# Scores of a short tile of 65 keys, made as two tiles of 64 columns, in a two-layer Perceiver kernel

## The reference

```python
q = (x @ Wq.T).reshape(B, N, H, D)
k = (y @ Wk.T).reshape(B, L, H, D)
v = (y @ Wv.T).reshape(B, L, H, D)
attn = jnp.einsum('bnhd,blhd->bhnl', q, k)
attn = jax.nn.softmax(SCALE * attn, axis=-1)
out = jnp.einsum('bhnl,blhd->bnhd', attn, v).reshape(B, N, C)
return out @ Wp.T + bp
```

## Time and profile before

| | |
|---|---|
| runs | 1291.32, 1292.21, 1295.77 us |
| median | 1292.21 us |
| profiled execution | 1284.61 us |
| its span (first to last instruction) | 1282.8 us |
| mean granted TensorE clock | 0.952 of full speed |
| busy | PE 90%, PEld 67%, DVE 49%, ACT 33%, POOL 26% |

### The profile page before, as it was taken

The page is one execution under the profiler, slowest core; times in us unless marked ns, Lnnn a source line. Parts: engine busy times, 40 slices in busy tenths (PEclk is TensorE's granted clock), DMA queues, the critical chain, the costliest instruction groups (busy, mean ns, idle before and its releaser), DMA issues.

```text
span 1282.8 us, 34101 instructions
## 1 busy us (share of the span) xinstructions
PE 1153.2 (90%) x15663; PEld 864.1 (67%) x15664; DVE 634.2 (49%) x977; ACT 426.2 (33%) x806; POOL 338.9 (26%) x366
## 2 busy tenths in 40 slices
PE   6888979796999999999999999999999999654986
PEld 3343434385788888887888887888887887442863
DVE  2011368546214555555555555556555545555286
ACT  1010152214224334334434434434334334221332
POOL 0000000104001333333333333233233233349122
PEclk9999989799999999999999999999999999766999
DMA  9999970633012002001002002002001003100000
GB/s 352 373 397 352 378 282 0 225 106 108 1 38 67 19 23 67 18 23 67 18 23 68 19 23 67 18 23 68 18 23 56 30 23 120 56 2 17 1 2 33
DMA packets 38879, 115.67 MB, mean 90 GB/s; under 512 B 2504, under 2 KB 3016, under 8 KB 34640
## 3 DMA queue, kind: packets, MB, share of 16 engines
q1 hardware_dynamic: 38736, 113.50, 24.6%
HBM read 112.44 MB, written 1.05 MB: 88 GB/s over the span
## 4 chain that ended last, share of the span: by engine, by line
PE 75%; DVE 8%; ACT 5%; SPq 5%; DMA 4%; issue 2%; POOL 0%; DVEq 0%; POOLq 0%; ACTq 0%
PE SB L389 45%; PE SC L1099 6%; PE SB L380 5%; PE SB L1129 4%; SPq L546 4%; DMA R<-in_ctx_t 2%; PE SB L925 2%; PE SC L1108 2%; ACT R L1615 1%; DMA R<-in_ctx 1%; PE SC L1092 1%; DVE LN L746 1%; PE SB L993 1%; PE SC L901 1%; PE SB L981 1%
## 5 line engine op out<-in xcount | busy, mean ns | idle before, releaser
L1615 ACT COPY R<-SB 64x512 f32<-64x512 f32 (+1 forms) x224 | 116.3, 519 | 202.0 <-PE SB L389 200.2
L1414 DVE TENSOR_REDUCE LN<-SC 128x64 f32<-128x768 f32 x128 | 116.6, 952 | 131.4 <-PE SC L1099 131.4
L389 PE MATMUL SB<-high,whigh 128*128 128x512 f32 (+2 forms) x512 | 180.3, 352 | 1.0 <-ACT Z L402 1.0
L389 PE MATMUL SB<-high,wlow 128*128 128x512 f32 (+2 forms) x512 | 178.8, 349 | 0.0
L389 PE MATMUL SB<-low,whigh 128*128 128x512 f32 (+2 forms) x512 | 177.3, 346 | 0.0
L389 PE MATMUL SB<-wlow,high 128*128 128x512 f32 (+1 forms) x416 | 167.5, 403 | 0.0
L389 PE MATMUL SB<-whigh,high 128*128 128x512 f32 (+1 forms) x416 | 165.3, 397 | 0.0
L389 PE MATMUL SB<-whigh,low 128*128 128x512 f32 (+1 forms) x416 | 165.2, 397 | 0.0
L686 POOL TENSOR_TENSOR added<-LN 128x768 f32<-128x768 f32 x32 | 58.6, 1831 | 285.4 <-ACT LN L1647 285.4
L686 POOL TENSOR_TENSOR added<-Z 128x768 f32<-128x768 f32 x32 | 58.7, 1833 | 273.5 <-ACT Z L1647 273.5
L1642 ACT COPY LN<-SC 128x128 f32<-128x128 f32 x64 | 17.0, 266 | 271.6 <-PE SC L1108 271.3
(11 more groups left out here) (224 smaller groups left out, 1872.3 us busy)
## 6 DMA issues: line engine op xcount, KB each, us to landing
R<-in_ctx_t SPq DMA_DIRECT2D x32, 1024.0 KB, 8.5
R<-in_ctx SPq DMA_DIRECT2D x8, 3072.0 KB
R<-in_ctx_t SPq DMA_DIRECT2D x16, 644.0 KB, 7.0
R<-in_f SPq DMA_DIRECT2D x4, 2048.0 KB, 15.4
R<-in_f SPq DMA_DIRECT2D x1, 8192.0 KB, 26.2
R<-in_ctx_t SPq DMA_DIRECT2D x12, 512.0 KB, 3.6
R<-in_Wk SPq DMA_DIRECT2D x3, 1024.0 KB, 11.0
R<-in_Wv SPq DMA_DIRECT2D x3, 1024.0 KB, 13.2
```

What stands on the lines that cost most here:

```text
L389: last = pe.matmul(out_, lhs[a][:, k, :], rhs[b][:, k, :], start=n == 0, stop=n == 3 * NC - 1)
L1414: inc(dve.tensor_reduce(tops[:, r * T:(r + 1) * T], sc_head[:, :, r, 0:6 * T].rearrange("p g (a q) -> p q g a", q=T), AX.XY, ALU.max), "ha ...
L1615: last = act.copy(keys[nu][64 * half:64 * half + 64, pairs, first * P:first * P + full], src[:, :, 0:full])
```

## The change

The short tile's scores are made in two column halves, as the full tiles are: keys 0 to 63 of the tile go to partitions 0 to 63 of the bank, and 64 columns beginning with key 64 go to partitions 64 to 127. Of the second half one column is a key of this pair; the other 63 are what stands behind it in the buffer (the next pair's keys, or for the last pair the 64 words added at the end, which are zeroed once). Their results go to partitions 65 to 127, which nothing reads. The view `short_words` is the short keys with 64 words more, `sums_inv` moves by 64 words, and DVE's `nop` becomes the filling of those words.

```diff
--- before.py
+++ after.py
@@ -482,8 +482,10 @@
         sums = [Z[:, 1, 1664 + s_ * P:1664 + (s_ + 1) * P].rearrange("p (r q) -> p r q", q=T) for s_ in range(2)]
         ones = Z[:, 1, 1920:1952]
         added_halves = added[:, :].rearrange("p (r a q) -> p r a q", r=2, q=T)
-        sums_inv = view(free4 + 6144 + HP * MR, NC * T)
         short_keys = view(free4 + 6144, HP * MR, HP, MR)
+
+        short_words = view(free4 + 6144, HP * MR + T)
+        sums_inv = view(free4 + 6144 + HP * MR + T, NC * T)
 
         def at_half(t):
 
@@ -1089,8 +1091,10 @@
                         pe.wait_ge(sem("sub4"), 24 * b + 3 * x + 3)
                         for r in range(2):
                             rows = slice(64 * u + 32 * r, 64 * u + 32 * r + 32)
-                            pe.matmul(sc_half[u][0:MR, r, 6 * T:7 * T], short_keys[rows, x, :],
-                                      qb[rows, x, :], start=True, stop=True)
+                            for j in range(2):
+                                pe.matmul(sc_half[u][64 * j:64 * j + 64, r, 6 * T:7 * T],
+                                          short_words[rows, x * MR + 64 * j:x * MR + 64 * j + 64],
+                                          qb[rows, x, :], start=True, stop=True)
                         for a in range(6):
                             for j in range(2):
                                 for g in range(2):
@@ -1377,7 +1381,7 @@
             for n in range(RING4):
                 inc(dve.nop(), f"read4_{n}", 1 + (n < SKIP4))
             inc(dve.nop(), "o4_read")
-            inc(dve.nop(), "sub4", 3)
+            inc(dve.memset(short_words[:, HP * MR:], 0.0), "sub4", 3)
 
             def run4(steps, b, u):
                 at, before = at4(steps, b)
```

## The result

Six executions of the changed kernel took 1274.31 to 1283.45 us, median 1276.24. Six of the kernel before beside them took 1285.67 to 1295.86, median 1293.27. The ratio is 0.9886, with a 95% interval of 0.9848 to 0.9924: 14.7 us less, give or take 5. (The two medians as they stand lie 17.0 apart.) The forecast was 1285.8, and its range ended at 1279.5. The direction was right, and the 6.4 us forecast were less than half of the 14.7.

A forecast was written before the change was run, and what follows sets the result against it. TensorE's own order of work was taken to bound the kernel, with a latency chain in the last batch. 59 x 0.097 = 5.7 plus 5 x 0.145 = 0.7 made 6.4 us off 1292.21: 1285.8, range 1279.5 to 1291.

The forecast's parts named there:

- The pause belongs to the form: Score step: the 65th column puts short calls into another form, breaking overlap; 0.26 us to the first full call.
- The first full call uses one of them, so it waits for a whole fresh round all the same: Head of score step: first full call starts 0.165 us behind the first short one, not 0.262; gain 0.097 a step.
- the bounds of 4.8 to 11.7: All 64 score steps: gain between 59 x 0.075 + 5 x 0.07 and 59 x 0.176 + 5 x 0.27 us.
- The prediction's own sign of being wrong: Score step: the full tiles' 96 records taking longer than 1.25 us as a group would show rival 1.
- a stall that eats the gain: Later rounds of the score step: one more supply shortfall cancels the 0.097 us a step, 1292 us; 12%.
- The clock adds a spread of its own ... which I set at 2 us either way: TensorE's granted clock: its low stretches shift, spreading the time by 2 us either way, set from the runs' scatter.
- rival 4: Full tiles' first round: runs at the quick pace, another 0.05 us a step off, 1283 down to 1280; 20%.
- rival 1: Score step's later rounds: with 52 calls for 48 another supply shortfall eats the 0.097 us gain, 1292 us; 12%.
- rival 2: Between short and full tiles: the pause belongs to the short tile's place and stays, 0.8 us slower, 1293; 3%.
- rival 3: Head of each score step: column halves of one row group serialize, 0.66 us more a step, 42 us, 1334; 2%.
- The waits at batch starts: Score steps' waits for ACT at batch starts: 8.0 us in seven, forecast to stay unchanged.
- DVE's fill: Head of the stage: a 128 x 64 fill, 0.1 us once, hidden by DVE's 0.73 us wait for TensorE.

The follow-up runs named there:

- the changed order: Kernels with the change's four short calls, also column half by column half or behind the full tiles, against the kernel before: mean 1275.0 us over 14 executions.
- the other order: Changed kernel with its four short calls ordered column half by column half: median 1271.74 us, ratio to the kernel before 0.9886.
- 54 and 56 calls: Changed kernel with the short tile's second column half made twice (54 a step), median 1292.73 us, or all four short calls made twice (56), 1293.67.
- 50 calls: Changed kernel with only the short tile's first 64 keys, two short calls in place of four: median 1275.86 us, ratio to the kernel before 0.9923.

## Why the prediction was wrong

**The pause belongs to the form: right.** Four runs show it, the changed kernel and three more. 64 columns in the same place remove it, 65 behind the full tiles bring it along, 32 columns make another.

**"The first full call uses one of them, so it waits for a whole fresh round all the same": the step that failed first.** The full calls don't wait for the short ones as a group: first passes of both are interleaved, and the first full call starts 0.03 us behind the first short one, not 0.165. And no price per call or round could be read from the earlier trace rows, since what a call costs depends on how many there are (0.02 us each to reach 52, 0.06 to reach 54). The gain was sized at 0.097 us a step and measured 0.123; at the lower clock it was sized at 0.145 and measured 0.2. That makes 8.2 us instead of 6.4, inside the bounds of 4.8 to 11.7. The prediction's own sign of being wrong, full records that take longer than 1.25 us as a group, appeared too: they take 711.02 - 709.65 = 1.37 us now. But that is the interleaving, not a stall that eats the gain.

**"The clock adds a spread of its own ... which I set at 2 us either way": the step that put the result out of the range.** I took the low stretches as noise that both kernels share, worth 2 us. They don't share it: over 29 and 14 executions of one comparison the half clock took up to 67.5 us from the kernel before and up to 61.4 from the changed order, so up to 6.1 of 15.0 us. In single traces low stretches cost up to 4.8 us in the stage (three of 1.6), and the end differs by up to 10, where a longer low stretch makes DVE lose a race against POOL. Of the kernels run here, those with steps near 1.44 had the long end in five of six traces in which POOL was untouched, those with steps of 1.32 in none of four. The range should have been set by what a low stretch costs in rows of this kernel: the stretch at 784.90 was in the trace from the start. The starting value moved as well: beside the later runs the kernel before had medians of 1291.82, 1286.13 and 1287.28 us, where the prediction started from 1292.21.

**Rivals.** The larger gain (rival 4) had the right side, and its reason, a fresh start paid only once, fits the interleaved first passes. The stall of supply (rival 1) has a counterpart in the stair between 52 and 54 calls, just beyond the change. Had the tile needed six calls, all of the gain would have been gone: 1.447 us. The break did not stay (rival 2). The serialized column halves (rival 3), and with them the rule of the Trainium skill (TensorE: Matmul & The Clock Gate, "The mechanism") on weight loads in one row group, have the traces against them: all eight records of the four calls have started within 0.13 us, and the other order takes as long.

**The rest.** The waits at batch starts stayed at 8.0 us, and DVE's fill costs nothing that could be seen.

**What stays open.** Why the low stretches fall as they do, and with that the cause of some 6 of the 14 us. It is shown that the mean granted clock differs between kernels whose steps differ by a tenth of a microsecond, and that kernels with the old length and without the change of form have the lower clock and the long end too. It isn't shown that the length is the cause: at batch starts 54 and 56 calls had few low stretches (1 of 9), as the changed kernel has, and 50 calls had either end. Why 54 and 56 calls are 5 to 6 us slower than the kernel before, with steps of the same length, is open as well.

## What to carry to other kernels

Calls of one form flow into each other, and a single one whose column count falls into another form stops the flow twice, at some 0.15 us each time (a record's 0.22 less the 0.07 of overlap); one column too many can be cheaper as a second, mostly empty call of the common form. Find what added calls cost by running neighbours in number: here two more calls cost 0.04 us in one place and 0.12 in the next. And where a chain of latencies meets a half-speed clock or a second engine on the same memory, look at two or three traces of the same kernel, and at the granted clock of every execution, before setting a range: here the same kernel's last part took 136 or 146 us.

## What the runs showed of the hardware

- A change between 32\*64 and 32\*65 and one between 32\*64 and 32\*32 cost about the same: 0.26 us from the first of two calls of 65 columns to the next form, and 0.24 for each single call where 64 and 32 columns alternate.
- The cost of 48, 50, 52, 54 and 56 small calls in a row: 1.185, 1.265 or 1.298 (by the half of the rows that the two added calls use), 1.323, 1.447, 1.440 us.
- Calls on the two column halves of the same 32 rows run at once: eight records of four such calls have started within 0.13 us.
- A DVE operation of 0.55 us took 1.6 to 8.0 us beside POOL operations. The one of 7.17 us outlasted the POOL operation that it met and the whole of the next. With POOL held back three of the four took 0.55 again, in both kernels.
- Low stretches of 3.4 us in the dense stage came behind batch starts at which TensorE had been idle for 1.6 us (one: 2.75), and not behind each of them: 9 of 15 with calls of 65 columns, 1 of 18 in the changed order.
